# Mamba layer of a four-layer tower on one core: rows of B and C through DRAM, B spread in fp32, one z moved into the scan

## The chip, the cores and the metric

The kernel runs on one core of a Trainium2 chip. The metric is the device time of one execution in microseconds. TensorE is called PE here, VectorE DVE, ScalarE ACT, GpSimd POOL, and the queue that issues the DMAs SP.

## The reference

Eight sequences of 512 tokens and 256 channels go through attention, a diagonal scan layer, a ternary feed-forward with a convolution, a Mamba layer and a ternary gated feed-forward, with a class token in front (513 tokens) after the first. What the change touches is the Mamba layer:

```python
xz = x @ W_in.T
x_val, z = jnp.split(xz, 2, axis=-1)            # 512 channels each
x_val = _silu(causal conv of 4 taps over x_val)
dt = jax.nn.softplus(x[:, :, :dt_rank] @ W_dt.T + b_dt)
Bm = x @ W_B.T                                   # 16 states
Cm = x @ W_C.T
def step(h, inp):
    dt_t, xv_t, B_t, C_t = inp
    dA = jnp.exp(dt_t[:, :, None] * A[None])
    h = dA * h + (dt_t * xv_t)[:, :, None] * B_t[:, None, :]
    return (h, jnp.einsum('bdn,bn->bd', h, C_t))
y = y * _silu(z)
return y @ W_out.T
```

## The kernel before

The program makes four turns over pairs of sequences (`PAIR` = 2, called batch 0 and 1). Channels lie on the partitions, tokens on the free axis, so the 512 inner channels are four tiles (`DT` = 4). Semaphores are written out by hand, every engine has its own instruction list, and each list is run strictly in its order. Products for the inputs go through four PSUM slots in turn: `plan_fills` (L94) lists the fills, and `fill` (L661) waits until the reader of the slot's previous fill is done. The order of the Mamba fills is: d0 to d3 (the time step) of both batches, bc of both, x0 to x3 of both, z0 to z3 of both.

Ahead of the scan, ACT makes the time step through Abs, Exp and Ln, and the first tap of each convolution (`first_tap`, L1149). DVE splits B and C into three bf16 parts (L1541 to L1552, tile `bcp`), rounds (L1230), adds three taps to each of eight tiles (L1565) and closes the time step (L1571). POOL adds two terms (L1736, L1739) and makes dt*x for both batches (L1743). The layer's normalisation in front of it ends on DVE at L1289.

The scan runs over 32 steps k = 16*batch + state, each of four tiles. The recurrence itself is one `tensor_tensor_scan` of 512 tokens for each tile, on DVE (L1631). For step k:

- PE spreads row k of B over 128 partitions into one PSUM bank, a bf16 product with a selecting matrix (`spread_b`, L913), and row k of C into another (`spread_c`, L918). ACT copies both to SBUF (`c_row`, `b_row`).
- DVE multiplies 3 or 2 tiles of dt*x with B from PSUM (`spread`, L1582), POOL the other 1 or 2 with B from SBUF (`spread_pool`, L1750). Three buffers hold the result.
- ACT writes the decays exp(dt*A) into two PSUM banks in turn. They are read by the four scans.
- POOL multiplies the four states with C (L1761, called the C product below; `hc_ready` counts it), into one of two buffers.
- PE adds the four tiles to y in four PSUM banks by fp32 products with the identity (`add_y`, L931, called the sum below).

DVE's list has, for step k, first the spread of step k+1 and then the four scans of step k. PE's list is:

```python
                spread_b(0)
                spread_c(0)
                spread_b(1)
                for k in range(PAIR * NS):
                    if k + 2 < PAIR * NS:
                        spread_b(k + 2)
                    if k + 1 < PAIR * NS:
                        spread_c(k + 1)
                    if k:
                        add_y(k - 1)
```

After the scan come a short tail, the gates with z (L1600), and the projection. ACT's instructions nearly all have line L1009, a helper, and PE's fills L667.

Of the kernel before, what the change touches and what calls it, by code (L numbers as in the profile page):

```python
# [14 lines left out]
F32 = mybir.dt.float32  # L15
BF16 = mybir.dt.bfloat16
# [44 lines left out]
SETUP_POOL = 6  # L61
# [29 lines left out]
GU_ORDER = ["G0", "G1"] + [n for c in range(HT - 2) for n in (f"G{c + 2}", f"U{c}")] + [f"U{HT - 2}", f"U{HT - 1}"]  # L91


def plan_fills():  # L94
# [36 lines left out]
    each(*[f"d{c}" for c in range(DT)])  # L131
    each("bc")
    each(*[f"x{c}" for c in range(DT)])
    each(*[f"z{c}" for c in range(DT)])
# [73 lines left out]
def build(nc, x, w, scratch, out):  # L208
    with ExitStack() as ctx:
# [19 lines left out]
        wbc = sb("wbc", [P, KT, 96])  # L229
# [3 lines left out]
        sel = sb("sel", [96, 32], BF16)  # L233
        ones96 = sb("ones96", [96, P], BF16)
        bc0 = sb("bc0", [96, PAIR, 32], BF16)
# [15 lines left out]
        bcp = sb("bcp", [96, PAIR, T + 1], BF16)  # L251
# [37 lines left out]

        def big_un(p):  # L290
            o = p * 2 * W8
            return big[:, o:o + KT * T].rearrange("p (c t) -> p c t", c=KT)

        def big_sq(p):
            o = p * 2 * W8 + KT * T
            return big[:, o:o + KT * T].rearrange("p (c t) -> p c t", c=KT)

        def big4(p, n):
            o = p * 2 * W8 + 2 * KT * T + n * DT * T
            return big[:, o:o + DT * T].rearrange("p (c t) -> p c t", c=DT)  # L300

# [30 lines left out]
        def c_row(i):  # L332
            o = 5 * W4 + (i % 2) * S
            return big[:, o:o + S]

        def b_row(i):
            o = 5 * W4 + 2 * S + (i % 2) * S
            return big[:, o:o + S]
# [33 lines left out]
        c_psum = psum[:, 6 * BANK:7 * BANK]  # L372
# [72 lines left out]
        bc_split = signal("bc_split")  # L445
# [7 lines left out]
        c_spread = signal("c_spread")  # L453
# [5 lines left out]
        c_copied = signal("c_copied")  # L459
        b_used = signal("b_used")  # L460
        b_copied = signal("b_copied")
# [50 lines left out]
        for p in range(PAIR):  # L512
# [23 lines left out]
            for c in range(DT):  # L536
                readers[f"x{c}", p] = (m_tap, 3 * (DT * p + c) + 3)
                readers[f"z{c}", p] = (z_silu, DT * p + c + 1)
                readers[f"d{c}", p] = (sp_pre, DT * p + c + 1)
            readers["bc", p] = (bc_split, 6 * p + 2)  # L540
# [10 lines left out]
        def _(sp):  # L551
# [17 lines left out]
            def turn(i, last):  # L569
# [45 lines left out]
                for m in range(len(MAX_GROUPS)):  # L615
# [4 lines left out]
                    if 1 <= m <= NG:  # L620
# [4 lines left out]
                        stack_quarter(m - 1, k_stack, K_PARTS, 2)  # L625
                if not last:
# [20 lines left out]
        def _(pe):  # L647
# [4 lines left out]
            def turn_products(i):  # L652
# [235 lines left out]
                for p in range(PAIR):  # L888
                    pe.wait_ge(ln_normed, q_of(3, p))
                    for c in range(DT):  # L890
                        fill(f"d{c}", p, [(wdt[:, c * P:(c + 1) * P], big_un(p)[:, 0])])
                for p in range(PAIR):
                    fill("bc", p, [(wbc[:, k], big_un(p)[:, k]) for k in range(KT)], rows=96)
                for p in range(PAIR):
                    for c in range(DT):
                        fill(f"x{c}", p, [(wx[:, k, c * P:(c + 1) * P], big_un(p)[:, k]) for k in range(KT)])
                for p in range(PAIR):
                    for c in range(DT):
                        fill(f"z{c}", p, [(wz[:, k, c * P:(c + 1) * P], big_un(p)[:, k]) for k in range(KT)])


                pe.wait_ge(z_silu, DT * PAIR)
                pe.wait_ge(bc_split, 6 * PAIR)
                pe.wait_ge(bc_first, 1)
                nc.tensor.matmul(c_psum[:, 0:PAIR * 32], ones96[:, :], bc0[:, :, :].rearrange("p b r -> p (b r)"),
                                 start=True, stop=True).then_inc(first_full, 1)

                def spread_row(k, r, o):

                    return nc.tensor.matmul(o, sel[:, r:r + 1].broadcast_to([96, P]), bcp[:, k // NS, 1:T],  # L910
# [935 lines left out]
```

## Time and profile before

| | |
|---|---|
| median of 3 runs | 2689.73 us (2687.26 to 2691.68) |
| the profiled execution | 2690.58 us, span 2688.8 us |
| busy in the span | PE 78%, DVE 77%, ACT 48%, POOL 45% |
| mean granted PE clock | 0.928 of full speed |
| L1631 scans on DVE | 614.2 us busy, 512 instructions |
| L1761 C products on POOL | 560.0 us busy, 124 instructions |
| L931 sums on PE | 528.4 us busy, 992 records |

The page gives the busy share of each engine in 40 slices of the span; four like stretches, one for each turn, are seen in it, and in POOL's row the scans of the Mamba layer stand out:

```profile
PE   2898877777799886777779997677877998867786
DVE  6864869986885578997788467899687847789967
ACT  1564366553165436653327544566323744455632
POOL 1110259991211116997222110899521212289932
PEclk9999988998999998999899999899989999989898
```

The busy time of an engine is the union of its instructions' times. An fp32 product shows as two records for each piece of up to 512 columns. A row of the timeline merges like instructions that follow one another; what stands in brackets is the engine's idle time before it and what released it. In the chain of waits each piece is what the next one waited for.

### The profile page before, as it was taken

To read this page: it belongs to the slowest core of one execution; us is meant where nothing else is said; L and a number is where in the kernel's file an instruction comes from. 1 tells how busy PE (TensorE), PEld (TensorE's weight loads), DVE (VectorE), ACT (ScalarE), POOL (GpSimd) and SP (SyncE) were. 2 spreads that over 40 slices of the span, in tenths; PEclk is the share of its full clock that TensorE was granted. 3 is DMA by queue.
4 is the path that set the end of the run, shared out by engine and by line. 5 is a ranking of instruction groups with operands and counts; after the bars stand their busy time and mean duration, and the time that the engine had idled before them with its cause. 6 is when DMAs were issued, how large, how long until landed. Compare 5 with 4: busy or idle time off the path is not lost.

```text
span 2688.8 us, 24367 instructions
## 1 busy us (share of the span) xinstructions
PE 2102.5 (78%) x8636; PEld 1142.2 (42%) x8636; DVE 2080.8 (77%) x2361; ACT 1281.0 (48%) x1810; POOL 1211.9 (45%) x567
## 2 busy tenths in 40 slices
PE   2898877777799886777779997677877998867786
PEld 0226652235423664224542475322453246632254
DVE  6864869986885578997788467899687847789967
ACT  1564366553165436653327544566323744455632
POOL 1110259991211116997222110899521212289932
PEclk9999988998999998999899999899989999989898
DMA  5200000000120000000022000000003100000000
GB/s 177 86 13 0 1 0 0 0 0 1 68 84 1 1 1 0 0 0 0 1 86 65 1 1 0 0 0 0 0 1 114 37 1 1 0 0 0 0 0 16
DMA packets 41072, 51.26 MB, mean 19 GB/s; under 512 B 9072, under 2 KB 32368, under 8 KB 40944
## 3 DMA queue, kind: packets, MB, share of 16 engines
q1 hardware_dynamic: 40944, 49.62, 5.8%
q8 instruction: 72, 1.18, 0.2%
q14 instruction: 56, 0.46, 0.1%
HBM read 26.25 MB, written 10.49 MB: 14 GB/s over the span
## 4 chain that ended last, share of the span: by engine, by line
PE 48%; DVE 23%; POOL 14%; issue 8%; ACT 6%; DMA 1%; SPq 0%; POOLq 0%; DVEq 0%; ACTq 0%
PE psum L667 15%; PE psum L931 12%; POOL big L1761 10%; PE psum L796 5%; POOL big L1750 4%; PE psum L770 3%; PE psum L784 3%; DVE mid L1297 3%; ACT big L1009 3%; DVE mid L1565 3%; PE psum L729 2%; ACT mid L1009 2%; PE psum L803 2%; PE psum L686 2%; DVE mid L1230 2%
## 5 line engine op out<-in xcount | busy, mean ns | idle before, releaser
L931 PE MATMUL psum<-big,ident 128*128 128x512 f32 x992 | 528.4, 682 | 202.1 <-POOL big L1761 201.8
L1631 DVE TENSOR_TENSOR_SCAN big<-psum,b,big 128x512 f32<-128x512 f32 x512 | 614.2, 1262 | 0.0
L1009 ACT ACTIVATE big<-psum 128x1024 f32<-128x1024 f32 (+2 forms) x592 | 450.4, 777 | 302.3 <-PE psum L784 160.2
L1761 POOL TENSOR_TENSOR big<-big 128x2048 f32<-128x2048 f32 x124 | 560.0, 4517 | 22.3 <-DVE big L1631 22.3
L1009 ACT ACTIVATE psum<-mid,aneg 128x512 f32<-128x512 f32 x512 | 353.9, 692 | 265.0 <-DVE big L1631 265.0
L931 PEld LDWEIGHTS psum<-big,ident 128*128 128x128 f32 x992 | 203.9, 216 | 485.1 <-POOL big L1761 264.3
L1399 DVE TENSOR_REDUCE negmax<-psum 128x1 f32<-128x512 f32 x512 | 318.2, 679 | 26.7 <-PE psum L770 25.5
L1750 POOL TENSOR_TENSOR big<-mid,big 128x512 f32<-128x512 f32 (+1 forms) x128 | 222.2, 1736 | 19.9 <-ACT big L1009 19.9
L770 PE MATMUL psum<-mid 96*128 96x512 bf16 x512 | 189.2, 383 | 24.8 <-DVE negmax L1399 23.7
L784 PE MATMUL psum<-mid 98*128 98x512 bf16 x512 | 186.0, 382 | 21.0 <-ACT big L1009 10.8
L1009 ACT ACTIVATE mid<-mid 128x513 f32<-128x513 f32 (+2 forms) x112 | 97.9, 899 | 201.6 <-DVE mid L1283 201.4
L1582 DVE TENSOR_TENSOR big<-mid,psum 128x1536 f32<-128x1536 f32 (+1 forms) x128 | 187.4, 1464 | 5.8 <-PE psum L910 5.7
L1726 POOL TENSOR_TENSOR big<-big,mid 128x513 f32<-128x513 f32 x40 | 51.6, 1303 | 283.8 <-ACT big L1009 283.8
L1009 ACT ACTIVATE mid<-psum 128x513 f32<-128x513 f32 x96 | 57.6, 600 | 235.6 <-PE psum L729 203.4
L1704 POOL TENSOR_TENSOR lsum<-lsum,onorm 128x512 f32<-128x512 f32 x20 | 25.4, 1270 | 316.3 <-ACT onorm L1009 316.3
L1775 POOL TENSOR_TENSOR big<-big,mid 128x513 f32<-128x513 f32 x40 | 47.8, 1204 | 234.4 <-ACT big L1009 234.0
L796 PE MATMUL psum<-big,mid 128*32 128x512 f32 x1024 | 132.8, 611 | 13.1 <-ACT osb L1009 13.1
L729 PE MATMUL psum<-ident,tok 128*128 128x128 f32 (+1 forms) x640 | 113.3, 326 | 24.9 <-DVE tok L1322 15.7
L674 PE MATMUL psum<-w 128*128 128x512 bf16 x560 | 129.4, 379 | 0.0
L910 PE MATMUL psum<-bcp,sel 96*128 96x512 bf16 x256 | 82.4, 399 | 59.3 <-ACT big L1009 54.8
L770 PEld LDWEIGHTS psum<-mid 96*128 96x128 bf16 x512 | 49.7, 97 | 170.4 <-DVE negmax L1399 118.5
L729 PEld LDWEIGHTS psum<-ident,tok 128*128 128x128 f32 (+1 forms) x640 | 101.3, 231 | 45.1 <-DVE tok L1322 22.6
(185 smaller groups left out, 3434.6 us busy)
## 6 DMA issues: line engine op xcount, KB each, us to landing
mid<-mid SPq DMA_DIRECT2D x192, 64.0 KB, 2.6
mid<-scratch SPq DMA_DIRECT2D x192, 64.0 KB, 2.2
scratch<-big SPq DMA_DIRECT2D x4, 1536.0 KB, 6.1
out<-hres SPq DMA_DIRECT2D x8, 513.0 KB, 5.3
big<-in_x SPq DMA_DIRECT2D x8, 512.0 KB, 4.5
big<-in_w SPq DMA_DIRECT2D x2, 1024.0 KB, 6.3
big<-in_wg SPq DMA_DIRECT2D x1, 1024.0 KB, 10.0
big<-in_wu SPq DMA_DIRECT2D x1, 1024.0 KB, 11.9
```

Source lines behind the costliest of these rows:

```text
L667: mm = nc.tensor.matmul(o[:, a:b], lhs, rhs[:, a:b], start=(n == 0), stop=(n == len(products) - 1))
L729: mm = nc.tensor.matmul(o[:, t0:t0 + n], tok[0:n, p, which, c:c + 1].broadcast_to([n, P]), ident[0:n, 0:n], start=True, stop=True)
L770: nc.tensor.matmul(unit(("S", h, t)), q_stack[0:ROWS_MAX, h % H, t * P:(t + 1) * P], k_stack[0:ROWS_MAX, h % H, :], start=True, stop=True) ...
L784: mm = nc.tensor.matmul(st_unit(v)[:, t % 2], k_stack[0:KROWS, h % H, t * P:(t + 1) * P], q_stack[0:KROWS, h % H, :], start=True, stop=True)
L796: mm = nc.tensor.matmul(pv_bank[32 * j:32 * j + 32, :], vaug[:, g // NG, t, HG * (g % NG) + j], probs[:, g % 2, j, t], start=(t == 0), sto ...
L931: mm = nc.tensor.matmul(y_psum[:, c], ident[:, :], st(1, k)[:, c], start=(n == 0), stop=(n == NS - 1))
L1009: return nc.scalar.activation(o, a, func, **kw)
L1399: V.tensor_reduce(negmax[:, m % 2, k:k + 1], unit(("S", h, t)), AX_X, ALU.max, negate=True).then_inc(unit_free, 1)
L1582: V.tensor_tensor(st(0, k)[:, 0:m], mid4(k // NS, 3)[:, 0:m, 1:T], b_psum.unsqueeze(1).broadcast_to([P, m, S]), ALU.mult).then_inc(b_used, 1)
L1631: V.tensor_tensor_scan(st(0, k)[:, c], a_psum(DT * k + c), st(0, k)[:, c], b0[:, p, n, c:c + 1], ALU.mult, ALU.add).then_inc(scanned, 1)
L1750: G.tensor_tensor(st(0, k)[:, m:DT], mid4(k // NS, 3)[:, m:DT, 1:T], b_row(k).unsqueeze(1).broadcast_to([P, DT - m, S]), ALU.mult).then_in ...
L1761: G.tensor_tensor(st(1, k), st(0, k), c_row(k).unsqueeze(1).broadcast_to([P, DT, S]), ALU.mult).then_inc(hc_ready, 1)
```

## The change

- B and C are kept in fp32 as 32 rows (`bc_rows`) and no longer split. DVE copies them from PSUM; SP stores them to DRAM (`bc_dram`) and, for each step, loads one row of B and one of C to all 128 partitions, into four buffers each (`ROWS`). POOL reads B and C there, and the spread of C by PE and the two copies by ACT are gone.
- PE spreads B for DVE by an fp32 product of the 32 rows with a column of the identity. DVE reads it in the same PSUM bank as before. PE's order in the scan is new: B of step k+1 ahead of the sum of step k-1.
- z of batch 1: its first token is made ahead of the scan, the other 512 inside, one tile in each of the steps 3, 6, 9 and 12, copied by ACT; its Silu follows behind the last decay.
- The fills of the layer are in a new order, batch 0 first, and ACT's and DVE's lists ahead of the scan follow it. dt*x of batch 1 is made by DVE instead of POOL.
- Some tiles lie elsewhere in SBUF; the matrix `sel` and its setup on POOL are gone.

```diff
+MAMBA_FILLS = [(f"d{c}", 0) for c in range(DT)] + [("x0", 0), ("x1", 0)] + [(f"d{c}", 1) for c in range(DT)] \
+    + [("x2", 0), ("x3", 0), ("bc", 0), ("bc", 1), ("x0", 1), ("x1", 1)] + [(f"z{c}", 0) for c in range(DT)] \
+    + [("x2", 1), ("x3", 1)]
+Z_STEPS = (3, 6, 9, 12)
+ROWS = 4
...
+                    sp.wait_ge(bc_copied, p + 1)
+                    sp.dma_start(bc_dram[p], bc_rows(p)).then_inc(bc_stored[p], 16)
+                for k in range(PAIR * NS):
+                    p, n = divmod(k, NS)
+                    if k == 0:
+                        sp.wait_ge(bc_stored[0], 16)
+                    if k == 2:
+                        sp.wait_ge(dt_ready, PAIR)
+                    if k == NS:
+                        sp.wait_ge(bc_stored[1], 16)
+                    if k >= ROWS:
+                        sp.wait_ge(b_pool, k - ROWS + 1)
+                    sp.dma_start(b_row(k), bc_dram[p, n:n + 1, 1:T].broadcast_to([P, S])).then_inc(b_in[k % ROWS], 16)
+                    if k >= ROWS:
+                        sp.wait_ge(hc_ready, k - ROWS + 1)
+                    sp.dma_start(c_row(k), bc_dram[p, NS + n:NS + n + 1, 1:T].broadcast_to([P, S])).then_inc(
+                        c_in[k % ROWS], 16)
...
+                for name, p in MAMBA_FILLS:
+                    if name == "d0":
+                        pe.wait_ge(ln_normed, q_of(3, p))
+                    mamba_input(name, p)
+                first_token()
...
                 def spread_b(k):
                     if k:
-                        pe.wait_ge(b_copied, k)
-                    spread_row(k, k % NS, b_psum).then_inc(b_spread, 1)
-                def spread_c(k):
-                    if k:
-                        pe.wait_ge(c_copied, k)
+                        pe.wait_ge(b_used, k)
+                    r = k % NS
+                    nc.tensor.matmul(b_psum, ident[0:2 * NS, r:r + 1].broadcast_to([2 * NS, P]),
+                                     bc_rows(k // NS)[:, 1:T], start=True, stop=True).then_inc(b_spread, 1)
+                def late_z(c):
+                    if c:
+                        pe.wait_ge(z_raw, c)
                     else:
                         pe.wait_ge(first_copied, 1)
-                    spread_row(k, NS + k % NS, c_psum).then_inc(c_spread, 1)
+                        pe.wait_ge(z_first, 1)
+                    for k in range(KT):
+                        mm = nc.tensor.matmul(z_psum, wz[:, k, c * P:(c + 1) * P], big_un(1)[:, k, 1:T],
+                                              start=(k == 0), stop=(k == KT - 1))
+                    mm.then_inc(z_full, 1)
...
                 spread_b(0)
-                spread_c(0)
-                spread_b(1)
                 for k in range(PAIR * NS):
-                    if k + 2 < PAIR * NS:
-                        spread_b(k + 2)
                     if k + 1 < PAIR * NS:
-                        spread_c(k + 1)
+                        spread_b(k + 1)
                     if k:
                         add_y(k - 1)
+                    if k in Z_STEPS:
+                        late_z(Z_STEPS.index(k))
...
-                            if c == 1:
-                                if k >= 2:
-                                    act.wait_ge(hc_ready, k - 1)
-                                act.wait_ge(c_spread, k + 1)
-                                run(c_row(k), c_psum, ACT.Copy).then_inc(c_copied, 1)
-                                if k + 1 < PAIR * NS:
-                                    copy_b(k + 1)
+                            if c == 2 and k in Z_STEPS:
+                                zc = Z_STEPS.index(k)
+                                act.wait_ge(z_full, zc + 1)
+                                run(mid4(1, 1)[:, zc, 1:T], z_psum, ACT.Copy).then_inc(z_raw, 1)
+                nc.scalar.preload_act_table(ACT.Silu)
+                act.wait_ge(z_raw, DT)
+                for c in TAIL_ORDER:
+                    run(mid4(1, 1)[:, c, 1:T], mid4(1, 1)[:, c, 1:T], ACT.Silu).then_inc(z_late, 1)
+                load_ln_exp()
...
+                def copy_bc(p):
                     wait_full(dve, "bc", p)
-                    V.tensor_copy(dst, ps).then_inc(bc_split, 1)
...
+                    V.tensor_copy(bc_rows(p), slot("bc", p, 2 * NS)).then_inc(bc_copied, 1)
+                    dve.wait_ge(bc_copied, p + 1)
+                    affine2(bc0[:, p], ident[0:2 * NS, 0:2 * NS], bc_rows(p)[:, 0:1], None, ALU.mult).then_inc(bc_first, 1)
...
+                taps(0, 0)
+                taps(0, 1)
+                round_up(0)
+                taps(0, 2)
+                taps(0, 3)
+                for p in range(PAIR):
+                    copy_bc(p)
+                round_up(1)
+                taps(1, 0)
+                taps(1, 1)
+                steps_of(0)
+                taps(1, 2)
+                taps(1, 3)
+                first_sums()
+                steps_of(1)
                 dve.wait_ge(dt_ready, PAIR)
+                dve.wait_ge(m_silu, DT * PAIR)
+                V.tensor_tensor(mid4(1, 3), mid4(1, 2), mid4(1, 0), ALU.mult).then_inc(dtx_ready, 1)
...
-                    pool.wait_ge(dt_ready, p + 1)
-                    pool.wait_ge(m_silu, DT * (p + 1))
-                    G.tensor_tensor(mid4(p, 3), mid4(p, 2), mid4(p, 0), ALU.mult).then_inc(dtx_ready, 1)
+                pool.wait_ge(dt_ready, 1)
+                pool.wait_ge(m_silu, DT)
+                G.tensor_tensor(mid4(0, 3), mid4(0, 2), mid4(0, 0), ALU.mult).then_inc(dtx_ready, 1)
```

## Rows read from the trace of the kernel before

**Rows 1.** The page, part 1: busy us, share of the span, instructions.

```profile
PE 2102.5 (78%) x8636; PEld 1142.2 (42%) x8636; DVE 2080.8 (77%) x2361; ACT 1281.0 (48%) x1810; POOL 1211.9 (45%) x567
```

**Rows 2.** Durations ns (min/median/max) and starts; the last row from the page.

```profile
L1631 DVE TENSOR_TENSOR_SCAN big<-psum,b,big x128: 1254/1258/1279, 397.9 to 593.2; 128x512 f32<-128x512 f32 x128
...
L931 PE MATMUL psum<-big,ident x992: 590/592/1222, 407.3 to 2579.9; 128*128 128x512 f32 x199
...
L1750 POOL TENSOR_TENSOR big<-mid,big 128x512 f32<-128x512 f32 (+1 forms) x128 | 222.2, 1736 | 19.9 <-ACT big L1009 19.9
```

**Rows 3.** Stretches of the first turn: busy us by engine, PE clock, DMA.

```profile
342.00:398.00 56.00, 42.86 (x180) 33.80 (x180) 39.07 (x53) 35.95 (x46) 31.33 (x7) 0.91 0.00 0
...
398.00:597.00 199.00, 141.54 (x303) 54.87 (x304) 195.85 (x161) 121.12 (x188) 192.74 (x63) 0.89 0.00 0
```

**Rows 4.** Chain of waits ahead of the first scans: start us, length us.

```profile
342.28 9.02 PE psum L667 x40
...
351.33 0.70 DVE bcp L1541
...
358.63 2.28 DVE big L1230 x2
...
378.78 8.93 PE psum L667 x40
...
388.35 1.28 ACT L1013
...
393.57 1.77 DVE big L1582
```

**Rows 5.** Timeline, scan steps 1 to 4: start us, length us, idle before.

```profile
409.13 4.52 POOL L1761 TENSOR_TENSOR big<-big 128x2048 f32<-128x2048 f32 x1 [0.63 <-DVE big L1631]
...
413.70 3.70 PE L931 MATMUL psum<-big,ident 128*128 128x512 f32 x8 [0.20 <-POOL big L1761]
...
414.80 1.73 DVE L1582 TENSOR_TENSOR big<-mid,psum 128x1536 f32<-128x1536 f32 x1
...
415.54 0.58 ACT L1009 ACTIVATE big<-psum 128x512 f32<-128x512 f32 x1
...
416.44 4.80 DVE L1631 TENSOR_TENSOR_SCAN big<-psum,b,big 128x512 f32<-128x512 f32 x4
...
420.32 5.40 PE L931 MATMUL psum<-big,ident 128*128 128x512 f32 x8 [2.44 <-POOL big L1761]
...
421.16 1.19 DVE L1582 TENSOR_TENSOR big<-mid,psum 128x1024 f32<-128x1024 f32 x1
```

**Rows 6.** Timeline behind the first turn's last scan.

```profile
595.95 5.29 PE L931 MATMUL psum<-big,ident 128*128 128x512 f32 x8 [2.91 <-POOL big L1761]
...
605.60 0.69 DVE L1600 TENSOR_TENSOR mid<-psum,mid 128x512 f32<-128x512 f32 x1 [9.94 <-PE psum L957]
```

**Rows 7.** DMA issues: count, KB each, median us to landing.

```profile
mid<-scratch SPq DMA_DIRECT2D x192, 64.0 KB, 2.2
...
big<-in_x SPq DMA_DIRECT2D x8, 512.0 KB, 4.5
...
wq<-in_wq SPq DMA_DIRECT2D x1, 256.0 KB, 14.2
```

**Rows 8.** Two lines' instructions, all turns.

```profile
L1743 POOL TENSOR_TENSOR mid<-mid x8: 4492/5506/6521, 381.4 to 2367.0; 128x2052 f32<-128x2052 f32 x8
...
L1605 DVE TENSOR_TENSOR bxc<-first x8: 160/1312/2474, 390.0 to 2371.5; 128x16 f32<-128x16 f32 x8
```

**Rows 9.** Timeline of the inputs, first turn.

```profile
341.00 2.37 DVE L1289 TENSOR_TENSOR big<-big,mid 128x1026 f32<-128x1026 f32 x2 [4.42 <-ACT mid L1009]
...
346.77 1.91 ACT L1009 ACTIVATE mid<-mid 128x2052 f32<-128x2052 f32 x1
...
360.82 17.91 DVE L1565 SCALAR_TENSOR_TENSOR mid<-psum,vec,mid 128x512 f32<-128x512 f32 x24
...
378.64 4.92 DVE L1571 SCALAR_TENSOR_TENSOR mid<-mid,big 128x2052 f32<-128x2052 f32 x2
```

More of the change, by code:

```diff
@@ L58 @@
 NVEC = _n
-SETUP_POOL = 6
+SETUP_POOL = 2
 SETUP_DVE = 6 + 5 + 2 + 15 + 1
@@ L130, in plan_fills @@
     ln(3)
[L131 to L134, printed above, removed]
+    while len(order) % 4:
+        order.append(None)
+    order.extend(MAMBA_FILLS)
     while len(order) % 4 != 2:
@@ L444, in build @@
         z_silu = signal("z_silu")
-        bc_split = signal("bc_split")
+        z_first = signal("z_first")
+        z_full = signal("z_full")
+        z_raw = signal("z_raw")
+        z_late = signal("z_late")
+        bc_copied = signal("bc_copied")
+        bc_stored = [signal(f"bc_stored{p}") for p in range(PAIR)]
+        b_in = [signal(f"b_in{n}") for n in range(ROWS)]
+        c_in = [signal(f"c_in{n}") for n in range(ROWS)]
         sp_pre = signal("sp_pre")
@@ L897, in turn_products @@
[L897 to L906, printed above, removed]
@@ L1162, in _, with silu @@
-                nc.scalar.preload_act_table(ACT.Silu)
-                for c in range(DT):
-                    first_tap(1, c)
-                    act.wait_ge(m_tap, 3 * c + 3)
-                    run(mid4(0, 0)[:, c], mid4(0, 0)[:, c], ACT.Silu).then_inc(m_silu, 1)
-                for c in range(DT):
+                def silu(p, c):
+                    act.wait_ge(m_tap, 3 * (DT * p + c) + 3)
+                    run(mid4(p, 0)[:, c], mid4(p, 0)[:, c], ACT.Silu).then_inc(m_silu, 1)
+                for c in range(DT):
+                    step_input(0, c)
@@ new lines, in _, with silu_z @@
+                absolute(0)
+                first_tap(0, 0)
+                first_tap(0, 1)
+                exponential(0)
+                for c in range(DT):
+                    step_input(1, c)
+                logarithm(0)
+                first_tap(0, 2)
+                absolute(1)
+                first_tap(0, 3)
+                exponential(1)
+                first_tap(1, 0)
+                logarithm(1)
+                nc.scalar.preload_act_table(ACT.Silu)
+                def silu_z(c):
@@ L1168, in _ @@
                     wait_full(act, f"z{c}", 0)
                     run(mid4(0, 1)[:, c], slot(f"z{c}", 0), ACT.Silu).then_inc(z_silu, 1)
-                    act.wait_ge(m_tap, 3 * (DT + c) + 3)
-                    run(mid4(1, 0)[:, c], mid4(1, 0)[:, c], ACT.Silu).then_inc(m_silu, 1)
-                for c in range(DT):
-                    wait_full(act, f"z{c}", 1)
-                    run(mid4(1, 1)[:, c], slot(f"z{c}", 1), ACT.Silu).then_inc(z_silu, 1)
+                first_tap(1, 1)
+                silu(0, 0)
@@ new lines, in _ @@
+                silu(0, 1)
+                silu_z(0)
+                silu(0, 2)
+                silu_z(1)
+                silu(0, 3)
+                silu_z(2)
+                silu_z(3)
+                silu(1, 0)
+                first_tap(1, 2)
+                silu(1, 1)
+                first_tap(1, 3)
+                act.wait_ge(first_full, 1)
+                run(mid4(1, 1)[:, :, 0], z_psum[:, 2 * PAIR * NS:2 * PAIR * NS + DT], ACT.Silu).then_inc(z_first, 1)
+                run(first[:, :, :].rearrange("p b r -> p (b r)"), z_psum[:, 0:2 * PAIR * NS], ACT.Copy).then_inc(
+                    first_copied, 1)
@@ L1175, in _ @@
+                silu(1, 2)
+                silu(1, 3)
                 load_ln_exp()
[L1177 to L1179 removed]
                 act.wait_ge(dt_ready, PAIR)
[L1181 to L1187 removed]
@@ L1189, in _ @@
-                copy_b(0)
                 for p in range(PAIR):
```

191 lines of the change are left out of this document (84 added, 107 removed).

## The prediction

> **What bounds the kernel now.** I read the busy times of the whole span first [rows 1]: PE 78%, DVE 77%, POOL 45%, ACT 48%. No engine is full, so the question goes to the stages. The scans of L1631 lie in one block of 128 for each of the four turns; in the first turn the block starts at 397.9 us and its last scan at 593.2 [rows 2]. The stretches of the first turn [rows 3] show two different worlds. From 398 to 597 DVE is busy 195.85 of 199 us and POOL 192.74: both are full, PE (141.5) and ACT (121.1) are not. From 342 to 398, where the inputs of this layer are made, no engine is full: PE 42.9 of 56, DVE 39.1, ACT 36.0, POOL 31.3. There the chain of waits tells what counts [rows 4]: 9.0 us of PE (the d and bc products), then DVE's splitting of B and C from 351.33 to 358.6, DVE's taps (L1565) up to 378.74, the z products (8.9 us), an ACT table load, the first tokens, and the first spread of B at 393.57. The scan block is 197 of these 252 us, so I weigh it first.
>
> A scan step on DVE is one spread of B (1.73 or 1.19 us by record) and four scans (4.80) [rows 5]. The block lasts from 397.9 to 594.5 (its last scan is 1.26 long [rows 2]), 196.6 us for 32 steps: **6.14 us a step**. A POOL step is the C product, 4.52 [rows 5], and its share of B, 1.74 on average [rows 2], 6.25 by records that overlap a little. DVE and POOL are level; there is no spare time in either.
>
> **The change in the scan: who waits for PE.** The C row and POOL's B row come from DRAM. ACT loses two copies a step (0.58 us each [rows 5]), which saves nothing on the path, ACT being 61% busy there. The rows are 256 KB each; DMAs of 64 KB land in 2.2 us and of 512 KB in 4.5 [rows 7], so I take 3 us (an estimate between the two; the upper end 14.2 us is the slowest 256 KB load in the crowd at the start [rows 7]). A row is asked for when the C product four steps back is done, and used three and more steps later, 18 us or more. Hidden at both ends, and on SP too: behind these DMAs is queued only the load of the next turn's x, which waits for the end of the turn's last quantiser anyway. POOL reads the same sizes as before.
>
> The term that decides is PE's order. Before, iteration k of PE issues B product k+2 and then sums y of step k-1: B product j stands behind the sum of step j-4. After, it is B product k+1: **B product j stands behind the sum of step j-3.** DVE wants B product j just before the scans of step j-1. Lay this on the rows as they are [rows 5]. The scans of step 1 release POOL's C product of step 1, which runs from 409.13 to 413.65, its sum on PE 413.70 to 417.40. B product 4 would follow, and DVE wants it at 414.80. The sum of step 2 ends at 420.32 + 5.40 = 425.72, and DVE wants B product 5 at 421.16. So the new product is 3.5 and 5.5 us late once its own 0.9 us is added. Before, the product ran a whole step earlier, and that covered it.
>
> Its price is the loop: scans of k, C product of k, sum of k, B product k+3, spread k+3 on DVE, scans of k+2. The loop covers two steps. Scans 4.72 (start to next start, 416.44 to 421.16), POOL 4.52, the sum 3.70 right behind other PE work and 5.40 or 5.29 after 2.4 and 2.9 us of idle time [rows 5, 6], B product, spread 1.4 (1.73 and 1.19, of which the next scan hides 0.1, as 414.80 to 416.44 shows), hand-offs 4 times 0.05 to 0.08. For the B product: an fp32 product of 512 columns is two records, and eight records take 3.70, so 0.92 for two; at the half clock (1.2 instead of 2.4 GHz; records of 1.22 against 0.59 [rows 2]) up to 1.8. Sum with fast sums 4.72+4.52+3.70+0.92+1.40+0.25 = 15.5; with slow ones 17.2. PE's sums after a gap of 2.4 us and more start slow in the rows, and the gaps grow here, though only the first after a long gap is hit. I take the middle, **16.3 for two steps, 8.15 a step**, 2.0 more than now, for the 30 steps that come after the first two: **+60 us a turn** (ends: 7.75 and 8.6 a step, +48 and +74).
>
> **z of batch 1.** At steps 3, 6, 9 and 12 PE makes one z tile behind the sum, 2 fp32 products of 512 columns, 1.8 us (3.4 at half clock). ACT copies it between decays c=2 and c=3 of the same step, and queued behind this wait is the decay that DVE's fourth scan needs. From the end of the scans of step 2: C product 4.6, sum 3.7 to 5.4, z 1.8, copy 0.6, decay 0.69, the last scan 1.18, handoffs 0.15: 12.7 to 14.4 until step 3 ends, against 8.15. That is 4.6 to 6.3 more, and a part comes back, since the next B product is then early. I take 5 each, **+20 us a turn** (ends 14 and 25). What it buys is the 4 z fills before the scan, below. Their Silu, moved behind the last decay (a table load of 1.28 [rows 4], four of about 0.6), has some 11 us before the gates that need it, of which the first starts at 605.60 [rows 6], and costs nothing.
>
> **The change before the scan.** Removed from DVE: 12 splitting steps and the B0 product, 351.33 to 358.6, for two copies and two tiny products (about 1.6 together). Removed from PE: 4 z fills of 1.8 us each, which stand alone on the chain from 378.78 on [rows 4]. Moved from POOL to DVE: one of two products dt*x (4.50 on POOL alone [rows 8]; 2.4 on DVE, as 1026 elements take 1.2 at L1289 [rows 9]). With x ahead of bc, taps can start when ACT has made the first tap: 346.8 (end of the four step inputs) + 1.9 + 0.8, 349.5 instead of 360.82. From there DVE has 17.9 of taps, 2.3 of rounding, 1.6, two dt steps of 2.46, the new product 2.4 and 0.9 of small ones [rows 4, 9]: 30.0, ending at 379.5. On top come waits in the new order: taps of x2 of batch 0 stand behind d2 and d3 of batch 1, whose slots wait for the taps of x0 and x1 (3.7); taps of x2 of batch 1 stand behind z2 and z3 (2.0). And a third: in the rows a POOL product takes 6.51 instead of 4.50 when it meets the dt step of DVE, and a DVE product of 16 elements 2.46 instead of 0.16 when it meets POOL [rows 8]. DVE's first sums will so meet POOL's dt*x of batch 0 (2.5). Together 387.7 against 393.57: **-6 us a turn** (ends -3 and -10). From the first spread to the first scan it is 4.1 against 4.3, no change.
>
> The Trainium skill, SBUF — State Buffer, section "SBUF: two separate sides", says that the port pair of DVE and GpSimd is an exclusive lock, taken by DVE operations with two SBUF inputs; rows 8 agree. By that page the moved product of batch 1 must queue against POOL as well, which speaks against moving it; without any such lock the section would end 5 us earlier.
>
> Setup: three GpSimd selects and 64 KB of weights less, all under the load of the weights. Nothing. After the scan the sums and projections are as before, about 0.
>
> **Sum.** +60 +20 -6 = +74 us a turn, four turns +296. The profiled execution took 2690.58 (span 2688.8 and 1.8 around it), so 2986.6; the median of the three runs, 2689.73, gives **2986**.
>
> **Rivals.** (a) The forecast, the loop through PE with stalls at z: 0.80, between 4*(48+14-10) = +208 and 4*(74+25-3) = +384, so 2898 to 3074. (b) PE comes in time after all and only the section before the scan changes: 4 times -6 to -10, 2650 to 2666. It needs C product, sum and B product within a scan step plus spread, 6.1; in the rows they are 9.1 at best, so it holds only if the sum could start before the whole C product is done, and nothing shows that. 0.07, the other side. (c) The loop runs at the full clock and ACT's wait at z is mostly absorbed: 4*(48+4-10) = +168, 2858. 0.07. (d) PE falls to the half clock for good, as it waits more: the sum 6.9, B product 1.8, the loop 19.6, 9.8 a step, 30*3.66+32-6 = +136 a turn, 3234. Against it: at such a pace PE would be busy 17.4 of 19.6, and in the rows it is granted 0.89 on average at a lighter load of 141.5 in 199 [rows 3]. 0.05. The last 0.01 is no change, where (b) and a little stalling cancel.
>
> The range holds (a) whole and reaches down towards (c): 2880 to 3075. A difference of 0.2%, 5.4 us, is what the measurement can tell; faster 0.07, same 0.01, slower 0.92.
>
> **What the profile after would show.** DVE idle before its spread (L1582's successor), released by a PE product of B, a few us in nearly every step; the block of 128 scans longer by 60 to 100 us; POOL no longer full; four steps of 12 us or more early in the block in which DVE waits for ACT and ACT for PE; the first scan of turn one near 392. If instead DVE stays at 98% in the block, (b) holds and my reading of PE's order is wrong. If DVE waits for POOL on the queue of DMAs, rows land too late, which I priced at nothing. If steps without z are at 7.7 or at 8.6, the clock of the sums was mis-sized, and I would look at the granted clock there.

## The result and the profile after

The changed kernel takes 3028.26 us (median of 4 runs, 3021.11 to 3029.68) against 2690.26: 1.1253 times the time before, 95% interval 1.1233 to 1.1273. The forecast was 2986 and the range 2880 to 3075. The page of the changed kernel, parts 1, 2 and 5 (in part 5: busy us, mean ns of one, idle time of the engine before them and who ended it):

```profile
span 3027.9 us, 24140 instructions
...
PE 2246.3 (74%) x8640; PEld 1172.3 (39%) x8640; DVE 2095.0 (69%) x2329; ACT 1156.7 (38%) x1582; POOL 1131.6 (37%) x559
...
PEclk9999967888999997778999998778889999777888
...
L982 PE MATMUL psum<-big,ident 128*128 128x512 f32 x992 | 606.6, 767 | 418.5 <-POOL big L1837 418.5
...
L1714 DVE TENSOR_TENSOR_SCAN big<-psum,b,big 128x512 f32<-128x512 f32 x512 | 616.0, 1263 | 128.5 <-ACT psum L1056 128.5
...
L1837 POOL TENSOR_TENSOR big<-big 128x2048 f32<-128x2048 f32 x124 | 517.0, 4169 | 464.0 <-DVE big L1714 464.0
...
L1668 DVE TENSOR_TENSOR big<-mid,psum 128x1536 f32<-128x1536 f32 (+1 forms) x128 | 188.8, 1475 | 253.7 <-PE psum L961 253.6
```

DVE's spread (L1668) now has 253.7 us of idle time before it, ended by PE's product of B (L961), where it had 5.8 before. The scans (L1714) have 128.5 us, ended by ACT's decays, where they had none, and POOL waits 464 us for the scans, where it waited 22. The same two stretches as in [rows 3]:

```profile
341.00:393.00 52.00, 37.41 (x166) 28.29 (x166) 39.43 (x43) 32.48 (x40) 24.71 (x7) 0.87 0.16 48
...
393.00:684.00 291.00, 185.91 (x318) 69.22 (x319) 197.54 (x161) 90.98 (x133) 179.79 (x63) 0.78 0.19 50
```

In the block of scans DVE is busy for 197.5 us as it was before (195.9), but now of 291. PE was granted 0.78 of its full clock there, in place of 0.89. Each turn falls into four parts, by the starts of the instructions in the two traces: the inputs (last normalisation product to first scan), the block, the tail (last scan to first gate), and all the rest (gate to the next turn's inputs).

| us a turn | before | after | difference |
|---|---|---|---|
| inputs | 56.9 | 53.6 (last turn 54.6) | -3.0 on average |
| block of 128 scans | 196.6 | 290.0 | +93.4 |
| tail | 11.1 | 9.5 | -1.6 |
| the rest | 394.1, 397.3, 393.8 | 390.8, 394.3, 387.1 | -4.3 |

Four blocks give +373.5, four times inputs and tail -18.5, the rest -16, together the 339 us between the two spans.

The loop, once around, by the timeline of the first turn (start us, length us, engine, line, idle time before it and who ended it): POOL's C product of step 20, PE's sum of step 20, the products of B for step 23, DVE's spread of step 23, and the scans of step 22.

```profile
592.79 4.51 POOL L1837 TENSOR_TENSOR big<-big 128x2048 f32<-128x2048 f32 x1 [3.23 <-DVE big L1714]
...
597.36 5.84 PE L982 MATMUL psum<-big,ident 128*128 128x512 f32 x8 [5.12 <-POOL big L1837]
...
603.12 1.12 PE L961 MATMUL psum<-big,ident 32*128 32x512 f32 x2
...
604.28 1.22 DVE L1668 TENSOR_TENSOR big<-mid,psum 128x1024 f32<-128x1024 f32 x1 [5.20 <-PE psum L961]
...
605.42 4.80 DVE L1714 TENSOR_TENSOR_SCAN big<-psum,b,big 128x512 f32<-128x512 f32 x4
```

The sum starts when POOL ends (597.36), runs at the lower clock level (1.2 GHz) for most of its 5.84 us (five of its eight records are 0.97 to 1.22 us long, the last three 0.59), the B product follows, and DVE, idle for 5.20 us, starts its spread at 604.28. The scans of step 22 follow. In the second half of the block, from step 21 on, the steps come in pairs of 6.4 and 10.5 to 11.1 us, 17.2 for two on average, where the prediction had 16.3 and 15.5 to 17.2 as ends.

A step with z (step 3 of the first turn):

```profile
419.59 5.97 PE L982 MATMUL psum<-big,ident 128*128 128x512 f32 x8 [5.24 <-POOL big L1837]
...
425.40 1.88 PE L972 MATMUL psum<-big,wz 128*128 128x512 f32 x4
...
427.31 0.60 ACT L1056 ACTIVATE mid<-psum 128x512 f32<-128x512 f32 x1 [8.10 <-PE psum L972]
...
427.81 1.29 ACT L1056 ACTIVATE psum<-mid,aneg 128x512 f32<-128x512 f32 x2
...
428.53 1.28 DVE L1714 TENSOR_TENSOR_SCAN big<-psum,b,big 128x512 f32<-128x512 f32 x1 [7.69 <-ACT psum L1056]
```

The sum of step 2 ends at 425.56, z follows on PE, ACT copies it at 427.31 after having waited for 8.1 us, then come the decays, and the fourth scan starts at 428.53, after 7.69 us in which DVE had nothing. The scans of step 2 ended at 415.65 and those of step 3 at 429.81: 14.2 us for the step.

Ahead of the scans, behind DVE's new product dt*x of batch 1:

```profile
382.19 2.30 DVE L1660 TENSOR_TENSOR mid<-mid 128x2052 f32<-128x2052 f32 x1
...
384.56 3.45 POOL L1826 TENSOR_TENSOR big<-mid,big 128x512 f32<-128x512 f32 x2 [4.95 <-DVE mid L1660]
...
384.70 1.22 DVE L1699 SCALAR_TENSOR_TENSOR mid<-mid,s 128x4 f32<-128x4 f32 x1
...
385.84 2.26 DVE L1696 TENSOR_TENSOR b<-mid,first 128x64 f32<-128x64 f32 x1
...
388.27 1.75 DVE L1668 TENSOR_TENSOR big<-mid,psum 128x1536 f32<-128x1536 f32 x1
...
390.08 2.07 PE L961 MATMUL psum<-big,ident 32*128 32x512 f32 x2 [11.88 <-DVE big L1668]
```

DVE's four small products (0.9 us alone) last from 384.52 to 388.23, since they meet POOL's shares of B at 384.56. The B product behind the first spread, that of step 1, takes 2.07 us, at the lower clock level (1.2 GHz), after PE had been idle for 11.88 us. The loads of the rows are hidden, as forecast:

```profile
big<-bc_rows SPq DMA_DIRECT2D x256, 256.0 KB, 3.8
```

### The profile page after: what moved, and what is told of

Read it like the earlier page. It is cut to its first block, busy times and chain, and to the rows that moved or that the text cites. A ratio compares the mean times of both kernels' runs of the same rounds, so it can differ in the third digit from the quotient of the medians.

```text
span 3027.9 us, 24140 instructions
## 1 busy us (share of the span) xinstructions
PE 2246.3 (74%) x8640; PEld 1172.3 (39%) x8640; DVE 2095.0 (69%) x2329; ACT 1156.7 (38%) x1582; POOL 1131.6 (37%) x559
## 4 chain that ended last, share of the span: by engine, by line
PE 31%; issue 29%; DVE 17%; POOL 15%; ACT 6%; DMA 1%; SPq 0%; POOLq 0%; DVEq 0%; ACTq 0%
PE psum L705 11%; POOL big L1837 7%; POOL big L1826 7%; PE psum L834 4%; PE psum L808 3%; PE psum L822 3%; ACT mid L1056 3%; DVE mid L1367 3%; ACT big L1056 2%; PE psum L767 2%; PE psum L841 2%; PE psum L724 2%; DVE mid L1300 2%; DVE big L1413 2%; DVE negmax L1469 2%
## 5 line engine op out<-in xcount | busy, mean ns | idle before, releaser
L982 PE MATMUL psum<-big,ident 128*128 128x512 f32 x992 | 606.6, 767 | 418.5 <-POOL big L1837 418.5
L1714 DVE TENSOR_TENSOR_SCAN big<-psum,b,big 128x512 f32<-128x512 f32 x512 | 616.0, 1263 | 128.5 <-ACT psum L1056 128.5
L1837 POOL TENSOR_TENSOR big<-big 128x2048 f32<-128x2048 f32 x124 | 517.0, 4169 | 464.0 <-DVE big L1714 464.0
L982 PEld LDWEIGHTS psum<-big,ident 128*128 128x128 f32 x992 | 234.4, 249 | 789.5 <-POOL big L1837 518.2
L1056 ACT ACTIVATE big<-psum 128x1024 f32<-128x1024 f32 (+1 forms) x336 | 301.8, 921 | 247.3 <-PE psum L822 159.8
L1668 DVE TENSOR_TENSOR big<-mid,psum 128x1536 f32<-128x1536 f32 (+1 forms) x128 | 188.8, 1475 | 253.7 <-PE psum L961 253.6
L1826 POOL TENSOR_TENSOR big<-mid,big 128x512 f32<-128x512 f32 (+1 forms) x128 | 215.6, 1686 | 20.2 <-DVE mid L1660 20.2
L822 PE MATMUL psum<-mid 98*128 98x512 bf16 x512 | 186.1, 383 | 20.6 <-ACT big L1056 10.5
L1056 ACT ACTIVATE mid<-psum 128x513 f32<-128x513 f32 (+2 forms) x100 | 58.1, 581 | 353.1 <-PE psum L767 209.3
L961 PE MATMUL psum<-big,ident 32*128 32x512 f32 x256 | 150.8, 670 | 51.6 <-DVE big L1668 51.6
L1056 ACT ACTIVATE mid<-mid 128x513 f32<-128x513 f32 (+3 forms) x128 | 107.2, 866 | 180.5 <-DVE mid L1353 175.4
L767 PE MATMUL psum<-ident,tok 128*128 128x128 f32 (+1 forms) x640 | 119.1, 338 | 26.0 <-DVE tok L1392 16.5
L1367 DVE TENSOR_REDUCE mid<-big 128x513 f32<-128x4104 f32 x16 | 117.8, 7360 | 0.3
```

Source lines behind the costliest of these rows:

```text
L767: mm = nc.tensor.matmul(o[:, t0:t0 + n], tok[0:n, p, which, c:c + 1].broadcast_to([n, P]), ident[0:n, 0:n], start=True, stop=True)
L822: mm = nc.tensor.matmul(st_unit(v)[:, t % 2], k_stack[0:KROWS, h % H, t * P:(t + 1) * P], q_stack[0:KROWS, h % H, :], start=True, stop=True)
L982: mm = nc.tensor.matmul(y_psum[:, c], ident[:, :], st(1, k)[:, c], start=(n == 0), stop=(n == NS - 1))
L1056: return nc.scalar.activation(o, a, func, **kw)
L1367: V.tensor_reduce(mid1(p, 6), a.rearrange("p c t -> p t c"), AX_X, ALU.max, apply_absolute_value=True).then_inc(absmax_part, 1)
L1714: V.tensor_tensor_scan(st(0, k)[:, c], a_psum(DT * k + c), st(0, k)[:, c], b0[:, p, n, c:c + 1], ALU.mult, ALU.add).then_inc(scanned, 1)
```

## The experiments

The ratios below are against the kernel before, run again on the same chip; it took 2688.85, 2689.60 and 2688.92 us on the three chips. The experiments stand in the order in which they ran. Blocks, inputs and tails are measured as in the table above.

### B two ahead again

```diff
                 spread_b(0)
+                spread_b(1)
                 for k in range(PAIR * NS):
-                    if k + 1 < PAIR * NS:
-                        spread_b(k + 1)
+                    if k + 2 < PAIR * NS:
+                        spread_b(k + 2)
```

> The changed kernel with one thing undone: PE again issues the product of B two steps ahead (B of step k+2, then the sum of step k-1). B stays fp32, the rows still come from DRAM, z is still inside. If the order on PE is the cause, the steps without z fall from 8.57 us (17.15 for two in the second half of the block) to the 6.14 of before, the four z steps stay at 13 to 14 us, since ACT still waits for z there: a block of 196.6 + 4 x 8 = 229 us instead of 290, 2785 us in all. Rival: what costs is the fp32 product itself (1.1 us for 0.4) or the loads of the rows, not the order; then it stays near 3000.

Measured: 2763.69 us, 1.0276 (1.0256 to 1.0297). The block is 223.4 us instead of 290.1; the inputs stay at 53.8, the tail falls from 9.5 to 8.1. So 67 of the 93 us of each block come from one line of PE's order, with the product still in fp32 and the rows still from DRAM. The z step is what is left:

```profile
410.01 3.62 DVE L1715 TENSOR_TENSOR_SCAN big<-psum,b,big 128x512 f32<-128x512 f32 x3
...
416.72 1.88 PE L972 MATMUL psum<-big,wz 128*128 128x512 f32 x4
...
418.63 0.60 ACT L1057 ACTIVATE mid<-psum 128x512 f32<-128x512 f32 x1 [6.63 <-PE psum L972]
...
419.85 1.28 DVE L1715 TENSOR_TENSOR_SCAN big<-psum,b,big 128x512 f32<-128x512 f32 x1 [6.22 <-ACT psum L1057]
```

Step 2 ends at about 408.4 and step 3 at 421.1, 12.7 us: the sum ran at full clock this time. Two more of the four steps take as long, and one 14.3; with 13 to 14 each I had expected a block of 229. The fourth scan still waits for 6.22 us behind ACT's copy of z.

### ACT's copies of z two steps later

```diff
-                            if c == 2 and k in Z_STEPS:
-                                zc = Z_STEPS.index(k)
+                            if c == 2 and k - 2 in Z_STEPS:
+                                zc = Z_STEPS.index(k - 2)
```

> The changed kernel with ACT's four copies of z two steps later (steps 5, 8, 11, 14), so that ACT no longer waits for them in front of a decay. If the wait on ACT makes the z steps 14.2 us long, they shrink to the length of their neighbours plus PE's z product of 1.9, which stays between the sum and B: 4 x (14.2 - 8.6 - 1.9) = 15 us a turn less, 2968. Rival: it is the z product on PE that delays B, and ACT's wait is hidden behind it: 3028, no change.

Measured: 2944.29 us, 1.0948 (1.0926 to 1.097); the block 269.5 us. The wait on ACT was on the path, and more than I had worked out came back, 20.6 us a block for 15. The steps say where the 5 more come from. The twelve steps from 2 to 13 hold all four z products. They took 127.1 us in the changed kernel and 107.8 here, and six pairs of 17.2 would be 103. So a z with its copy in the same step cost 6.0 us, not the 5.6 of the expectation, and the product on PE alone costs 1.2, not 1.9.

### Both

> Both: B two steps ahead and the copies of z two steps later. If these two are the whole loss, DVE is full again (6.1 us a step, a block of 197), and what the change gains elsewhere is left: 3 us a turn ahead of the scans, 1.6 in the tail, up to 4.7 behind it: 2655 to 2678, faster than the kernel before. Rival: the 33 MB of rows each way or POOL's reading of them cost something too; then it ends above 2690.

Measured: 2661.91 us, 0.9893 (0.9875 to 0.9911), 27 us less than the kernel before on the same chip. The block's scans of the first turn, and a stretch of 197 us that starts a little ahead of it:

```profile
L1715 DVE TENSOR_TENSOR_SCAN big<-psum,b,big x128: 1253/1255/1278, 396.7 to 592.2; 128x512 f32<-128x512 f32 x128
...
393.00:590.00 197.00, 166.74 (x316) 61.08 (x317) 193.01 (x159) 87.73 (x129) 174.64 (x61) 0.89 0.28 74
```

The block is 196.8 us (396.7 to 592.2, and 1.3 for the last scan), that of before within 0.2, at a PE clock of 0.89 again. So the two waits are the whole loss of the block. The loads move 74 GB/s beside it (they read 67 MB more from DRAM in the whole execution, not the 33 of the expectation) and cost nothing that shows. POOL is busy for 174.6 of 197 us, where it was busy for 192.7 of 199 before: half of its C products take 3.81 us here instead of 4.51, of which below. That could hide a price of the loads; the run with the rows at the other place settles it.

### The kernel before with B one ahead

```diff
                 spread_b(0)
                 spread_c(0)
-                spread_b(1)
                 for k in range(PAIR * NS):
-                    if k + 2 < PAIR * NS:
-                        spread_b(k + 2)
+                    if k + 1 < PAIR * NS:
+                        spread_b(k + 1)
```

> The kernel before with PE's order alone changed: the product of B one step ahead instead of two (B of step k+1, C of step k+1, then the sum of step k-1); bf16 parts, ACT copies and z as before. If the order is the cause, the loop of two steps is scans 4.7, C product 4.5, sum 3.7 to 5.9, B 0.4 to 0.6, spread 1.4, hand-offs 0.3: 15.1 to 17.4, so 2.0 a step more than now: 4 x 62 = 248, 2940 (2865 to 3000). Rival: only fp32 B makes it late: within 20 us of 2690.

Measured: 2949.12 us, 1.0966 (1.0944 to 1.0988); the block 265.2 us, 68.6 more. The order alone, in the kernel before, costs what undoing it saved in the changed one. The same picture in its rows, with a B product of bf16:

```profile
574.67 6.22 PE L931 MATMUL psum<-big,ident 128*128 128x512 f32 x8 [2.96 <-POOL big L1760]
...
580.73 0.60 PE L910 MATMUL psum<-bcp,sel 96*128 96x512 bf16 x2
...
581.15 1.22 DVE L1581 TENSOR_TENSOR big<-mid,psum 128x1024 f32<-128x1024 f32 x1 [4.76 <-PE psum L910]
...
394.00:660.00 266.00, 162.03 (x302) 63.54 (x302) 197.13 (x161) 122.27 (x190) 193.72 (x64) 0.79 0.00 0
```

The products of B and C take 0.60 us together, and still DVE is idle for 4.76 us, since it is the place of the product and not its length that is late. ACT's copies and POOL's 193.7 us are those of before.

### The B product twice

```diff
                     r = k % NS
+                    nc.tensor.matmul(b_psum, ident[0:2 * NS, r:r + 1].broadcast_to([2 * NS, P]),
+                                     bc_rows(k // NS)[:, 1:T], start=True, stop=True)
                     nc.tensor.matmul(b_psum, ident[0:2 * NS, r:r + 1].broadcast_to([2 * NS, P]),
                                      bc_rows(k // NS)[:, 1:T], start=True, stop=True).then_inc(b_spread, 1)
```

> The changed kernel with PE's product of B made twice for each step, into the same bank. If the loop of two steps runs through this product once, two steps take 0.9 to 1.1 us more, that is 0.5 a step, 16 us a turn, 3090 us in all. It also gives the share of the fp32 form: one more fp32 product costs what is read here, and the bf16 one of before is half of it. Rival: PE has time to spare, since it is idle for a third of the block; then nothing changes.

Measured: 3098.03 us, 1.1515 (1.1483 to 1.1547), 70 us more than the changed kernel. The blocks are 300.1, 300.1, 303.3 and 302.6 us, 11.5 more on average where 16 were expected; the other 24 us of the 70 lie outside them. So the product is on the path, at 0.37 us for each of 31 more. An fp32 product in place of a bf16 one, half of that by the records, costs some 6 us a block of the 93, no more (an estimate).

### The rows at another place

```diff
-            o = big.shape[1] - (4 - n) * S if n < 4 else ...
+            o = big.shape[1] - (4 - n) * S - 10 if n < 4 else ...
```

> A side question. In the changed kernel the C product on POOL takes 4.50 us at steps 0 and 1 of each four and 3.81 at steps 2 and 3, which read C from other buffers; those start at 24 bytes past a multiple of 32, the slow ones at a multiple of 64. Here the two slow pairs of rows are laid 40 bytes lower, so that they too start 24 past a multiple of 32. If the place of the row sets it, all C products take 3.81, the loop loses 0.35 us a two steps on average, 5 us a turn: 3008. Rival: what sets it is what runs beside POOL (DVE's spread, the DMAs into the rows); then 4.50 stays in half of them, and the time too.

Measured: 3015.35 us, 1.1208 (1.1178 to 1.1238). The C products of the changed kernel (ns min/median/max):

```profile
L1837 POOL TENSOR_TENSOR big<-big x124: 3805/4497/4527, 398.2 to 2911.1; 128x2048 f32<-128x2048 f32 x124
```

and of the run:

```profile
L1837 POOL TENSOR_TENSOR big<-big x124: 3802/3812/3827, 396.1 to 2895.3; 128x2048 f32<-128x2048 f32 x124
```

All of them take 3.81 us now, with the same DMAs and the same neighbours. The block is 286.6 us, 3.5 less.

### The small products first

The kernel with both waits undone, and one wait more on POOL, so that it starts its share of B when DVE's four small products are done:

```diff
                 pool.wait_ge(dtx_ready, PAIR)
+                pool.wait_ge(first_state, 3 * PAIR + 1)
                 spread_pool(0)
```

> The kernel with B two steps ahead and z copied later, and POOL's first share of B held until DVE's four small products ahead of the scan are done. In the changed kernel these, 0.9 us alone, last from 384.5 to 388.2 while POOL runs its share. If the port shared by DVE and GpSimd holds them, as in rows 8 of before, the first scan comes 2.5 to 3 us earlier in each turn: 2662 - 11 = 2651. Rival: POOL's share, now later, is late for the third scan and gives it back: 2662.

Measured: 2653.36 us, 0.9863 (0.9841 to 0.9885). The inputs take 50.8 us instead of 53.6 (in the last turn 51.8), as expected, and nothing is given back:

```profile
385.35 2.29 DVE L1661 TENSOR_TENSOR mid<-mid 128x2052 f32<-128x2052 f32 x1
...
387.68 0.26 DVE L1697 TENSOR_TENSOR b<-mid,first 128x64 f32<-128x64 f32 x1
...
387.98 0.26 DVE L1697 TENSOR_TENSOR b<-mid,first 128x64 f32<-128x64 f32 x1
...
388.51 3.40 POOL L1827 TENSOR_TENSOR big<-mid,big 128x512 f32<-128x512 f32 x2 [5.74 <-DVE mid L1661]
```

The four products run from 387.68 to 388.37, and POOL's share starts behind them.

### The same with the rows at the other place

> The same with the rows shifted as well. DVE is full in the block (196.8 us for 32 steps in the run with both parts undone), so a faster POOL gives little: 0 to 3 us a turn where POOL and DVE meet, 2640 to 2651. If POOL still bounds some steps, more than that.

Measured: 2638.57 us, 0.9802 (0.978 to 0.9823): 51 us less than the kernel before on the same chip, and the fastest of all. The block is 195.2 us, 0.8 less, the inputs are 50.8. Of the difference of 11.6 us between the spans of these two profiled runs, 4.9 lie ahead of the first inputs, in layers that the edit doesn't touch, of which below.

### The kernel before with its rows shifted

```diff
-            o = 5 * W4 + (i % 2) * S
+            o = 5 * W4 + 6 + (i % 2) * S
...
-            o = 5 * W4 + 2 * S + (i % 2) * S
+            o = 5 * W4 + 6 + 2 * S + (i % 2) * S
```

> The kernel before with nothing changed but the place of its C and B rows in SBUF, 24 bytes higher (they started at multiples of 64). If the place of the row sets POOL's time, its C products fall from 4.51 to 3.81 us there as well. POOL and DVE were level in the block (192.7 and 195.9 of 199 us), so the block can fall to DVE's own 195.9 and a little less: 2 to 4 us a turn, 2674 to 2682. Rival: the short C products belong to the DMAs or the layout of the changed kernel; then 4.51 and 2690 stay.

Measured: 2669.07 us, 0.9931 (0.9911 to 0.9951). Without any DMA of rows and with nothing else changed:

```profile
L1761 POOL TENSOR_TENSOR big<-big x124: 3804/3814/3830, 402.3 to 2546.9; 128x2048 f32<-128x2048 f32 x124
```

The block is 194.9 us, 1.7 less, the tail 7.4 instead of 11.1: 5.4 a turn, 22 in all. The expectation had the block and not the tail. The place of the row sets POOL's time. It also gives a fair comparison for the block: with all C products at 3.81 us it takes 194.9 us here, with bf16 products, ACT's copies and no loads, and 195.2 in the run before this one, with fp32 products, the loads and z inside. So together those cost 0.3 us a block.

### Which places are slow

```diff
-            o = big.shape[1] - (4 - n) * S if n < 4 else ...
+            o = big.shape[1] - (4 - n) * S - (13, 13, 12, 8)[n] if n < 4 else ...
```

> The kernel of the previous experiments (B two ahead, z copied later, small products first) with the two C rows of the slow pair laid at two different places: that of steps 0, 4, ... at 16 past a multiple of 32 bytes, that of steps 1, 5, ... at a multiple of 32 that is none of 64. The other two stay at 24 past. If any place off a multiple of 64 will do, all C products take 3.81; if a multiple of 32 is already slow, a quarter of them stays at 4.50; if a multiple of 16 is, a half. The rows of B of the slow pair start at 12 past a multiple of 32 here.

A single run took 2646.73 us. The first four C products:

```profile
394.95 4.51 POOL L1839 TENSOR_TENSOR big<-big 128x2048 f32<-128x2048 f32 x1 [6.25 <-DVE big L1715]
...
401.31 4.51 POOL L1839 TENSOR_TENSOR big<-big 128x2048 f32<-128x2048 f32 x1 [0.80 <-DVE big L1715]
...
407.94 3.81 POOL L1839 TENSOR_TENSOR big<-big 128x2048 f32<-128x2048 f32 x1
...
413.50 3.81 POOL L1839 TENSOR_TENSOR big<-big 128x2048 f32<-128x2048 f32 x1 [0.53 <-DVE big L1715]
```

Places are counted from the start of the tile `big`. At 16 past a multiple of 32 bytes the product takes 4.51 us, at a multiple of 32 it takes 4.51, at 24 past it 3.81, and so on through all 124. So the multiples of 16 bytes that were tried are slow. No other place was tried for a row of C.

### dt*x of batch 1 back on POOL

```diff
+                for p in range(PAIR):
+                    pool.wait_ge(dt_ready, p + 1)
+                    pool.wait_ge(m_silu, DT * (p + 1))
+                    G.tensor_tensor(mid4(p, 3), mid4(p, 2), mid4(p, 0), ALU.mult).then_inc(dtx_ready, 1)
...
-                V.tensor_tensor(mid4(1, 3), mid4(1, 2), mid4(1, 0), ALU.mult).then_inc(dtx_ready, 1)
```

> The fastest kernel so far (B two ahead, z later, small products first, rows shifted) with the product dt*x of batch 1 back on POOL, behind that of batch 0. On DVE it takes 2.3 us, on POOL 4.5; DVE's small products wait for it. If the two engines stand in line for the same port, nothing is won by having it on POOL: the first scan comes 2.2 us later and each turn with it, 2638 + 9 = 2647. Rival: the product on DVE queues behind POOL's dt*x of batch 0 and would be better placed on POOL; then 2638 or less.

Measured: 2658.07 us, 0.9881 (0.986 to 0.9902), 19.5 more than with the product on DVE. The inputs take 53.0 to 53.1 us a turn (54.1 in the last) instead of 50.8, the 2.2 expected:

```profile
377.94 2.29 DVE L1632 SCALAR_TENSOR_TENSOR mid<-mid,big 128x2052 f32<-128x2052 f32 x1
...
380.31 4.50 POOL L1819 TENSOR_TENSOR mid<-mid 128x2052 f32<-128x2052 f32 x1 [2.62 <-DVE mid L1632]
...
384.90 0.26 DVE L1695 TENSOR_TENSOR b<-mid,first 128x64 f32<-128x64 f32 x1 [4.67 <-POOL mid L1819]
```

DVE ends its time step at 380.23, POOL makes the product in 4.50, and DVE waits for 4.67. That is 10 us in four turns. Of the 16.5 us between the spans of the two profiled executions, 8.6 lie behind the gates, in the layers between two Mamba layers, of which below.

## Why the prediction was right, step by step

The path, PE's order and the wait on ACT at z, was right. That the number came within 43 us has some luck in it: the block came out 13.4 us a turn above the forecast (93.4 for 60 + 20) and the inputs 3 us, together +66 in four turns, and 23 us that nobody had forecast, in the tail and the rest, went the other way. Without them the time would have been some 3051, still inside the range.

- **The order on PE** was the decisive term, and it is shown from both sides: undone in the changed kernel it gives 67 us a block back, made alone in the kernel before it costs 68 to 69. The sum had +60 (48 to 74).
- **The length of the loop** was too small at 16.3: it is 17.2. The term mis-sized is the sum on PE with the product behind it. I took the middle between sums at the full and at the lower clock level. In the rows above the sum that closes the long step takes 5.84, and the B product 1.12, not 0.92. The steps pair up into a short and a long one, and it is the sum of the long one, behind 5.1 us of idle time, that lies on the path. The upper end, 17.2, was the right value, with a fast product of 0.92 in it; the slow one of 1.8, which the working names, was never added.
- **z**: 6.0 us for each of the four, by the twelve steps told above, where the sum had 5. The z steps themselves take 14.2 to 14.4 us. Moving ACT's copies gave 20.6 us a block.
- **The inputs**: -3.0 a turn instead of -6. Of the waits of the new order the first came (3.3 us of idle time for 3.7). The second, of 2.0, did not show (0.17), and DVE's first sums met nothing (0.34 and 0.19 us for the 2.5 put on them). Instead DVE's time step of batch 0 met POOL (5.36 us at 369.65, where that of batch 1 takes 2.28), so that the whole came 2.0 late at the first spread. The terms that were wrong are the place of the meeting, the first sums, and "0.9 of small ones": the four small products met POOL's share of B and took 3.7. Holding POOL back gave 2.8 us a turn. The rest is the B product ahead of the first scan, 2.07 at the lower clock, which made 5.1 us from first spread to first scan out of the 4.1.
- **The Trainium skill**, SBUF — State Buffer, section "SBUF: two separate sides", says that a DVE operation with two SBUF inputs and a GpSimd operation that reads SBUF exclude each other for the whole instruction. The traces agree: 2.26 us for a small product of 0.26, and 5.36 for a time step of 2.28. The conclusion that I drew from it, that it speaks against moving dt*x to DVE, did not hold: at 382.19 POOL was idle, so the product queued behind nothing; on DVE it takes 2.30 us and on POOL 4.50, and having it on POOL costs 2.2 us a turn.
- **The rows through DRAM** cost nothing that shows: they land in 3.8 us (3 expected), the block with both waits undone is as long as before, and with the rows of both kernels at the other place the two blocks are 195.2 and 194.9. ACT's copies that they save were worth nothing either.
- **Tail and rest** were forecast at 0 and are -1.6 and -4.3 a turn. What shortened the tail stays open: the place of the rows alone takes 3.7 us off it in the kernel before, but nothing in the changed kernel (9.7 for 9.5 with all rows at the other place). As for the rest, the feed-forward layer behind the scans has no change in its code. PE's 40 small products for the token rows, and a stretch around them, before:

```profile
633.58 8.61 PE L729 MATMUL psum<-ident,tok 128*128 128x128 f32 x40 [0.44 <-DVE tok L1322]
...
632.00:656.00 24.00, 19.72 (x131) 16.11 (x132) 15.12 (x29) 11.13 (x20) 7.61 (x7) 0.86 0.01 2
```

and after:

```profile
720.84 7.20 PE L767 MATMUL psum<-ident,tok 128*128 128x128 f32 x40 [0.44 <-DVE tok L1392]
...
719.00:742.00 23.00, 19.07 (x139) 15.26 (x137) 15.70 (x30) 11.64 (x22) 8.11 (x7) 0.93 0.01 2
```

The granted clock (the third number from the end) is 0.86 before and 0.93 after, and the same products take 8.61 and 7.20 us. Over all runs the rest of a turn takes 387 to 400 us, and within one kernel it differs by up to 8 us between turns. The mean granted clock goes with it: 0.94 in the longest, the first turn with dt*x back on POOL (399.9 us), 0.96 in the third turn of the changed kernel (387.1). What sets the level in a stretch whose code is the same wasn't tested. It is also why a difference of 10 us between two kernels can't be put down to the Mamba layer unless its own parts show it.

The rivals fall: (b) no stall, by DVE's 253.6 us of idle time before the spread; (c) z absorbed, by the experiment with the copies later; (d) the half clock for good, by 0.78 granted and sums of 3.70 in every second step. The 6.9 us that (d) took for a sum stand in no row; of the 128 sums in the trace of the changed kernel the longest takes 6.78.

## What to carry to other kernels

Where an engine runs its list strictly in order, count for each of its products behind which earlier item it stands, and follow the loop through all engines: a product that is issued one step later can cost several times its own length (2.1 us a step in the kernel before, where the products of B and C take 0.60 together), although each engine has idle time. Moving work into such a loop is cheap only where no engine waits for its result in front of something that the bound engine needs; put the wait where the result is two steps old. Undone in these two places, the changed kernel is 1.1% faster than the kernel before, and 2% with the two small edits. Part of this is the place of the rows and no merit of the change: the kernel before gains 0.7% by that alone. Against it, with all rows at that place, the fastest kernel is 1.3% ahead (0.9802 against 0.9931).

## What the runs showed of the hardware that I had not expected

- A GpSimd product of 2048 fp32 elements with a row of 512 repeated over four tiles takes 3.81 us instead of 4.51 if the row starts 24 bytes past a multiple of 32 instead of at a multiple of 16 (all 124 of them, in two kernels). Its smaller share of B on one tile falls from 1.28 to 1.10 us, that on two tiles stays at 2.20. In the kernel before this edit alone gives 0.7%. Why the place matters was not tested.
- The same layers, with unchanged code, differ by up to 8 us between turns of one kernel (399.9 and 392.3 with dt*x back on POOL), and the clock granted to PE differs with them (mean 0.94 and 0.95).
